# Four-layer gated cross-attention kernel, one core: the last mixture of experts of batches 1 and 2 by sorted pages of tokens instead of densely

## The chip, the cores and the metric

The kernel runs on one core of a Trainium2 chip, as one launch. The time is the device time of that core in microseconds. TensorE is written PE, its weight loads PEld, VectorE DVE, ScalarE ACT, GpSimd POOL and SyncE SP. TensorE is granted one of two clock levels, 1.2 or 2.4 GHz; the profile prints the mean grant as a share of the higher one.

## What is computed

Four batches (B = 4) of S = 512 tokens with D = 128 features pass through four layers; each adds a gated cross-attention and a gated feed-forward part. The change touches the feed-forward part of the last layer, here called moe_3: a mixture of 64 experts of which each token uses six, and a shared expert.

```python
x = x + jnp.tanh(g_ffn[3]) * _L3_ffn_ref(_layernorm(x, axis=-1), ...)

def _moe_forward(...):                       # HIDDEN 128, INTER 64, E 64, K 6, G 8, TG 4
    shared = jax.nn.silu(x @ sg_w.T) * (x @ su_w.T) @ sd_w.T
    scores = jax.nn.sigmoid(x @ gate_w.T) + gate_bias
    group_scores = scores.reshape(T, G, E // G).max(axis=-1)
    ...                                      # keep the 4 best groups of 8 experts
    topk_w, topk_i = lax.top_k(masked_scores, K)
    topk_w = topk_w / (topk_w.sum(axis=-1, keepdims=True) + 1e-08)
    comb = jnp.zeros((T, E), x.dtype).at[jnp.arange(T)[:, None], topk_i].add(topk_w)
    h = jax.nn.silu(jnp.einsum('th,eih->eti', x, eg_w)) * jnp.einsum('th,eih->eti', x, eu_w)
    routed = jnp.einsum('eti,ehi,te->th', h, ed_w, comb)
    return shared + routed
```

## The kernel before

The program is a sequence of blocks; at a block's end all engines meet. In a block each engine has its own instruction stream, written in Python as a generator that yields step numbers. `interleave` (L691) merges the stream of the main work with those of side works: after the main work yields step n, every side whose next step is due at n or earlier goes on. So a side's instructions stand in program order between those of the main work, on every engine, and an engine that waits in a side's instruction also holds up the main work queued behind it.

After the first layers come, for each batch b, the blocks `attention_2` (L1524) and `attention_2f` (L1904). The rest of layer 2 and the attention of layer 3 is `back` (L2173): a chain of 33 steps in which PE, ACT, DVE and POOL take turns on one PSUM bank. For batches 0 to 2 it runs in the block `backs` (L2684), all three side by side, between the two parts of the attention of batches 2 and 3. For batch 3 it is a side of the third moe_3 block, one step per item. Its norms use POOL for the power of -0.5.

`moe_3` (L2454) is dense. It treats the shared expert and 32 pairs of experts as 33 items. For each item PE makes the gate and the up product for all 512 tokens (`up`, L2479, two matmuls with 512 columns), ACT takes the silu (L2528), DVE multiplies by the up product (`used_3`, L2566) and by the token's share for that expert, which is zero where it isn't chosen (`gated_3`, L2574), and PE adds the down product into one bank (`down`, L2498, four matmuls with 128 columns). The shares come from a routing prologue on DVE (L2535 to L2556), are turned by PE (L2495), written to the DRAM tensor `gates3` and read back broadcast over the partitions (`spread_gates_3`, L2431, SP's queue). Expert weights are loaded anew for each batch in eight chunks of gate, up and down (`load_experts_3`, L2421); the first four chunks of the next batch are loaded at the end of a block. The next batch's layernorm is a side at steps 32 to 34 (`norm_ahead`, L642), and PE is kept busy with products that nobody reads (`keep_turning`, L630).

Layer 1's mixture is already done by pages: `route_1` (L1048) sorts two batches' tokens by expert on chip (ranks by matmuls with triangular and all-one matrices), POOL scatters the normed rows to DRAM (L1182, one indirect DMA for 128 rows), `pages_1` (L1196) loads pages of 128 rows, each of one expert, and uses that expert's weights at an address held in a register (L1253, L1270); `combine_1` (L1468) gathers the results back (L1476).

Of the kernel before, what the change touches and what calls it, by code (L numbers as in the profile page):

```python
# [44 lines left out]
FRONT_SMALL = 884  # L45
HID = 4
# [7 lines left out]
ROUND_MAGIC = 1.5 * 2.0 ** 22  # L54
LN2 = float(np.log(2.0))
# [7 lines left out]
def flamingo_kernel(nc, a, at, early_at, out):  # L63
    with ExitStack() as ctx:
# [17 lines left out]
        found_1 = [ctx.enter_context(nc.semaphore(f"rows_found_{b}")) for b in range(B)]  # L82

# [190 lines left out]
        back_2 = dict(**back_wide(region_b), **back_rest(region_a, 0))  # L274
        back_3 = dict(**back_wide(region_c), **back_rest(region_a, 1280))
        back_w2, back_w3 = back_norm(region_a, 2560), back_norm(region_a, 3840)
# [72 lines left out]

        hid = part(turned, 0, [P, HID, F1])  # L350
# [42 lines left out]
        made_1 = [nc.dram_tensor(f"made_1_{g}", (PAGES * P, D), FP32, kind="Internal").ap() for g in range(2)]  # L393

# [1129 lines left out]
        def attention_2(k, b, combined=None, last=None):  # L1524
# [75 lines left out]
            with nc.Block() as block:  # L1600
                @block.sync
                def _(sp):
                    clear_set(sp, 1 - k % 2)
                    if last:
                        last.sync(sp)

# [566 lines left out]
        def back(s, b, bk, bk_sum, w, f):  # L2173
# [217 lines left out]
            def gpsimd(pool):  # L2391
# [16 lines left out]
                 "hu", "hc", "y", "dve", "x", *LOADS, *AHEAD)  # L2408

        def load_gate_3(sp, s, c):  # L2410
            sp.dma_start(eg3[:, c, :], a["eg3"][:, c, :]).then_inc((s.load0, s.load1, s.load2, s.load3)[c % 4], 16)  # L2411

        def load_up_3(sp, s, c):
            sp.dma_start(eu3[:, c, :], a["eu3"][:, c, :]).then_inc((s.load0, s.load1, s.load2, s.load3)[c % 4], 16)

        def load_down_3(sp, s, c):
            lo = ed3_lo + 4 * D * c
            sp.dma_start(ed3[:, 4 * c:4 * (c + 1), :].rearrange("p c d -> p (c d)"),
                         a["weights"][:, lo:lo + 4 * D]).then_inc((s.load0, s.load1, s.load2, s.load3)[c % 4], 16)

        def load_experts_3(sp, s, chunks):  # L2421

            loads = (s.load0, s.load1, s.load2, s.load3)
            for c in chunks:
                if c >= 4:
                    sp.wait_ge(loads[c % 4], 48 * (c // 4))
                load_gate_3(sp, s, c)
                load_up_3(sp, s, c)
                load_down_3(sp, s, c)

        def spread_gates_3(sp, s, s_next=None):  # L2431
# [5 lines left out]
            for n in range(4 * CH3):  # L2437
# [6 lines left out]
                if n % 4 == 1 and n // 4 < 4:  # L2444
                    load_experts_3(sp, s, (4 + n // 4,))
                if s_next and n in (18, 21, 24, 27):
                    sp.wait_ge(s.y, 17)
                    load_experts_3(sp, s_next, ((n - 18) // 3,))
# [5 lines left out]
        def moe_3(s, b):  # L2454
# [18 lines left out]
            def tensor(pe):  # L2473
# [5 lines left out]
                def up(i):  # L2479
# [4 lines left out]
                    else:  # L2484
                        c, at_row = (i - 1) // 4, P * ((i - 1) % 4)
                        if at_row == 0:
                            pe.wait_ge(loads[c % 4], 48 * (c // 4 + 1))
# [18 lines left out]
                for i in range(n_items + 2):  # L2506
# [6 lines left out]
                    if i == n_items + 1:  # L2513
# [76 lines left out]
            return record(tensor=tensor, vector=vector, scalar=scalar, gpsimd=gpsimd)  # L2590

# [79 lines left out]
        def attention_2f_then_moe_3(b, b_next):  # L2671
            k = next_block()
            s_next = sems(1 - k % 2, MOE_3)

            def early_loads(sp, s):
                sp.wait_ge(s.o, 3)
                for c in range(4):
                    load_gate_3(sp, s_next, c)
                sp.wait_ge(s.o, 4)
                for c in range(4):  # L2680
                    load_up_3(sp, s_next, c)
            attention_2f(k, b, xs[b_next], copy_xnt, None, early_loads)

        def backs():  # L2684
# [4 lines left out]
            s_ahead = sems(k % 2, AHEAD, s_of[-1])  # L2689
# [149 lines left out]
```

## Time and profile before

| | us |
| --- | --- |
| median of 3 runs (lowest to highest) | 1861.17 (1857.43 to 1866.37) |
| the profiled execution, its whole time | 1862.18 |
| its span, first to last instruction | 1860.4 |
| mean granted clock of PE in it | 0.948 |
| PE busy, of the span | 1671.0 (90%) |
| DVE busy | 1175.6 (63%) |
| ACT busy | 771.9 (41%) |
| POOL busy | 750.9 (40%) |

In the page of the profile, the second part cuts the span into 40 slices of 46.5 us and prints the busy share of each engine in tenths. The last nine slices are the four moe_3 blocks: PE at 9, POOL at 0, DMA at 3 to 6. The shares of busy time are for the whole span, the blocks are bound in different ways, and what the change is worth has to be read from its blocks.

### The profile page before, as it was taken

To read this page: it belongs to the slowest core of one execution; us is meant where nothing else is said; L and a number is where in the kernel's file an instruction comes from. 1 tells how busy PE (TensorE), PEld (TensorE's weight loads), DVE (VectorE), ACT (ScalarE), POOL (GpSimd) and SP (SyncE) were. 2 spreads that over 40 slices of the span, in tenths; PEclk is the share of its full clock that TensorE was granted. 3 is DMA by queue.
4 is the path that set the end of the run, shared out by engine and by line. 5 is a ranking of instruction groups with operands and counts; after the bars stand their busy time and mean duration, and the time that the engine had idled before them with its cause. 6 is when DMAs were issued, how large, how long until landed. Compare 5 with 4: busy or idle time off the path is not lost. (4 is left out here: it accounts for less than half of the span.)

```text
span 1860.4 us, 30824 instructions
## 1 busy us (share of the span) xinstructions
PE 1671.0 (90%) x10277; PEld 1113.9 (60%) x10277; DVE 1175.6 (63%) x3054; ACT 771.9 (41%) x1957; POOL 750.9 (40%) x976
## 2 busy tenths in 40 slices
PE   5755699899999899999999979699999999999999
PEld 4545377657756477565676654457756565656656
DVE  6857568867666477564775653757656555554655
ACT  2321254346537466273662643146627322232321
POOL 2441744347666287471874750026646100000000
PEclk7866799999999999999999988899999999999999
DMA  9010122100000000000000000000000564634352
GB/s 334 19 29 1 40 88 77 32 10 9 1 1 2 2 11 1 1 2 1 10 4 1 2 1 0 1 1 1 2 1 24 168 192 127 194 105 127 112 173 85
DMA packets 63964, 92.51 MB, mean 50 GB/s; under 512 B 11192, under 2 KB 29240, under 8 KB 63040
## 3 DMA queue, kind: packets, MB, share of 16 engines
q1 hardware_dynamic: 61760, 86.34, 15.1%
q0 software_dynamic: 2048, 4.20, 0.8%
q8 instruction: 85, 1.39, 0.3%
q14 instruction: 71, 0.58, 0.1%
HBM read 80.55 MB, written 9.96 MB: 49 GB/s over the span
## 5 line engine op out<-in xcount | busy, mean ns | idle before, releaser
L1617 POOL TENSOR_TENSOR rows<-rows,rinv 128x512 f32<-128x512 f32 x192 | 198.5, 1061 | 117.4 <-DVE rinv L1857 117.4
L2528 ACT ACTIVATE region_b<-psum 128x512 f32<-128x512 f32 x132 | 78.8, 597 | 259.4 <-PE psum L2490 259.4
L1781 ACT ACTIVATE rows<-psum,nmax 128x512 f32<-128x512 f32 x192 | 129.9, 682 | 123.5 <-DVE nmax L1850 123.4
L2502 PEld LDWEIGHTS psum<-region_c,region_b 128*128 128x128 f32 x1024 | 132.1, 192 | 56.8 <-issue 43.9
L2566 DVE TENSOR_TENSOR region_b<-region_b,psum 128x512 f32<-128x512 f32 x128 | 87.8, 686 | 123.7 <-ACT region_b L2528 121.3
L1849 DVE TENSOR_REDUCE lg<-psum 128x2 f32<-128x1024 f32 x128 | 155.7, 1216 | 3.3
L1966 POOL TENSOR_TENSOR rows<-rows,rinv 128x128 f32<-128x128 f32 (+2 forms) x192 | 127.1, 684 | 75.6 <-DVE rinv L2135 75.6
L2130 DVE TENSOR_REDUCE nmax<-psum 128x1 f32<-128x128 f32 (+3 forms) x256 | 113.7, 486 | 40.8 <-PE psum L2012 39.8
L1861 DVE COPY turned<-psum 128x512 f32<-128x512 f32 x128 | 88.2, 689 | 80.5 <-PE psum L1677 79.5
L1665 PE MATMUL psum<-region_a,region_b 64*128 64x256 f32 x1024 | 130.6, 392 | 5.9 <-ACT rows L1781 2.9
L2502 PE MATMUL psum<-region_c,region_b 128*128 128x128 f32 x1024 | 133.7, 276 | 1.7 <-DVE region_b L2574 1.7
L2489 PE MATMUL psum<-xnt,region_a 128*128 128x512 f32 x256 | 132.0, 597 | 0.0
L2490 PE MATMUL psum<-xnt,region_a 128*128 128x512 f32 x256 | 130.8, 592 | 0.0
L1698 PE MATMUL psum<-turned,region_a 128*64 128x256 f32 x1024 | 124.7, 386 | 0.4
L2009 PE MATMUL psum<-region_a,region_b 64*128 64x128 f32 (+2 forms) x896 | 104.5, 346 | 11.2 <-ACT rows L2082 5.3
L1665 PEld LDWEIGHTS psum<-region_a,region_b 64*128 64x128 f32 x1024 | 93.0, 187 | 28.7 <-ACT rows L1781 7.7
L1677 PEld LDWEIGHTS psum<-weights,rows 128*128 128x128 f32 x768 | 82.0, 140 | 44.8 <-issue 24.9
L1677 PE MATMUL psum<-weights,rows 128*128 128x128 f32 x768 | 103.3, 279 | 3.8 <-ACT turned L1790 2.4
L2082 ACT ACTIVATE rows<-psum,nmax 128x128 f32<-128x128 f32 (+2 forms) x192 | 96.0, 509 | 10.4 <-DVE nmax L2130 10.4
L1698 PEld LDWEIGHTS psum<-turned,region_a 128*64 128x64 f32 x1024 | 68.7, 137 | 47.0 <-issue 19.6
L1790 ACT ACTIVATE turned<-psum 128x512 f32<-128x512 f32 x128 | 76.5, 598 | 46.2 <-PE psum L1677 46.2
L616 POOL TENSOR_SCALAR rtmp<-mv 128x4 f32<-128x4 f32 x3 | 0.7, 227 | 223.7 <-DVE mv L609 223.7
(747 smaller groups left out, 3619.7 us busy)
## 6 DMA issues: line engine op xcount, KB each, us to landing
pt<-gates SPq DMA_DIRECT2D x128, 128.0 KB, 3.2
ysb<-gates SPq DMA_DIRECT2D x128, 128.0 KB, 3.5
region_a<-in_eg SPq DMA_DIRECT2D x32, 256.0 KB, 3.5
region_a<-in_eu SPq DMA_DIRECT2D x32, 256.0 KB, 3.6
region_c<-in_weights SPq DMA_DIRECT2D x32, 256.0 KB, 4.8
sorted<-kctx SPq DMA_DIRECT2D x2, 1536.0 KB, 14.6
region_b<-sorted SPq DMA_DIRECT2D x12, 256.0 KB, 3.5
made<-rows SPq DMA_DIRECT2D x12, 256.0 KB, 2.4
```

The lines of the kernel that those rows point to most:

```text
L1617: nc.gpsimd.tensor_tensor(row(u, j), row(u, j), rinv[:, 2 * u + j:2 * u + j + 1].broadcast_to([P, S]), ALU.mult).then_inc(s.pn, 1)
L1665: mm = nc.tensor.matmul(s_bank(u, j)[:, 256 * half:256 * (half + 1)], qtt[lo:lo + 64, p, P * t:P * (t + 1)], ktt[lo:lo + 64, p, 256 * half ...
L1677: mm = nc.tensor.transpose(turn_bank(place(n, i))[:, P * k:P * (k + 1)], row(u, j)[:, P * k:P * (k + 1)], ident[:, :])
L1698: nc.tensor.matmul(bank(7)[lo:lo + HD2, 256 * half:256 * (half + 1)], vtok[:, k, P * p + lo:P * p + lo + HD2], turned2[:, 2 * half + j, k, :],
L1781: nc.scalar.activation(row(u, j), s_bank(u, j), ACT.Exp, bias=nmax[:, 2 * u + j:2 * u + j + 1], accum_out=sum_column(u // T, u % T, j)).th ...
L1849: link(nc.vector.tensor_reduce(maxima(u // T)[:, both(u), 0], both_scores(u), AX.X, ALU.max, negate=True))
L1966: nc.gpsimd.tensor_tensor(head, head, rinv[:, 2 * u + j:2 * u + j + 1].broadcast_to([P, keys(u)]), ALU.mult).then_inc(s.pn, 1)
L2009: nc.tensor.matmul(s_bank(u, j)[:, cols], qtt[lo:lo + 64, p, P * t:P * (t + 1)], krot[lo:lo + 64, cols], start=(h == 0), stop=True, skip_g ...
L2130: nc.vector.tensor_reduce(nmax[:, 2 * u + j:2 * u + j + 1], s_bank(u, j)[:, 0:keys(u)], AX.X, ALU.max, negate=True).then_inc(s.mx, 1)
L2489: nc.tensor.matmul(bank(i % 2), wg, w.xnt[:, :], start=True, stop=True)
L2490: nc.tensor.matmul(bank(2 + i % 2), wu, w.xnt[:, :], start=True, stop=True).then_inc(s.g, 1)
L2502: mm = nc.tensor.matmul(bank(7)[:, P * t:P * (t + 1)], htb[:, i % 2, P * t:P * (t + 1)], wd, start=(i == 0 and t == 0), stop=(i == n_items ...
```

## The change

Batches 1 and 2 no longer have a dense moe_3 block each. Their 1024 tokens are sorted by expert into pages of 128 rows: `QUADS_3 = (6*8 + 64)//4 = 28` groups of four pages, always all 112 pages, whatever the routing.

- The block `backs` gets on SP the loads of batch 0's eight gate chunks, and at its end (steps 33 and 35) batch 0's layernorm as a side. That layernorm leaves the last `attention_2f`.
- Batch 0's dense moe_3 moves ahead of the last `attention_2`, directly behind `backs`. Its side is `route_3`: layernorm of 8 token tiles, logits, choice of six of 64, ranks and starts of the experts' pages, 48 indirect DMAs that scatter the normed rows to `sorted_3`, the owners of the pages, the shares, and the shared expert for both batches.
- SP copies zero rows into `sorted_3` during batch 1's `attention_2` (`fill_rows_3`, 14464 rows of 512 B, and 128 rows more).
- The last `attention_2f` gets the loads of the first three groups of pages and of all gate and up chunks; the next block begins with the loads of all down chunks.
- The block `pages_3` has batch 3's `back` as a side, slowed by `paced` so that its step n is due at page 2n (one step for every two pages), and batch 3's layernorm at pages 67 to 70.
- The last block is batch 3's dense moe_3, with the expert weights still resident and without loads; its side `combine_3` gathers the made rows by 48 indirect DMAs and adds them by 48 DVE operations at steps 14 to 19 and 27 to 32.
- `back_2` and `back_3` get other places in `region_a`; `keep_turning` leaves the last block.

```diff
+GROUP_3 = (1, 2)
+GT3, K6 = 2 * T, 6
+QUADS_3 = (K6 * GT3 + E3) // 4
+PAGES_3 = 4 * QUADS_3
...
+        def route_3(s, bk, bk2):
...
+            def vector(dve):
+                link = chained(dve, s.chain)
+                yield 0
...
+                for j, rows in enumerate(tiles):
+                    nc.vector.bn_stats(stats_3[:, j, :], rows).then_inc(s.stat, 1)
...
+                yield 1
+                dve.wait_ge(s.rstd, 2)
+                for j, rows in enumerate(tiles):
+                    nc.vector.tensor_scalar(xn_3[:, j, :], rows, mv_3[:, j, 0:1], rstd_3[:, j:j + 1],
+                                            ALU.subtract, ALU.mult).then_inc(s.xn, 1)
...
+                    link(nc.vector.tensor_tensor(share_of, from_3, best_3[:, :, k:k + 1].broadcast_to(wide), ALU.is_equal))
+                    link(nc.vector.tensor_tensor(share_of, share_of, comb_3, ALU.mult))
+                    yield (17, 18, 20, 22, 23, 24)[k]
+                    link(nc.vector.tensor_reduce(shares_3[:, k, :], share_of, AX.X, ALU.add))
...
+                pool.wait_ge(s.slots, 1)
+                for j in range(GT3):
+                    for k in range(K6):
+                        nc.gpsimd.indirect_dma_start(sorted_3[:, :], bass.IndirectOffsetOnAxis(ap=slots_3[:, j, k:k + 1], axis=0),
+                                                     xn_3[:, j, :], None).then_inc(scattered_3, 16)
...
+        def pages_3(s, s_late):
+            gate_up = region_a[:, 0:2 * CH3 * 512].rearrange("p (a n) -> p a n", a=2)
+            TURN_LAG, DOWN_LAG = 2, 3
...
+                def up(q, j):
+                    if j == 0:
+                        owners[q] = nc.tensor.value_load(owner_quad3[0:1, q:q + 1], min_val=0, max_val=E3 ** 4 - 1)
+                        pe.wait_ge(s.xtc, q + 1)
...
+                        if q == 0:
+                            pe.wait_ge(s.up_in, 16 * 2 * CH3)
+                    at_expert = (owners[q] // E3 ** j) % E3 * I3
+                    mm = nc.tensor.matmul(up_bank(q)[:, P * j:P * (j + 1)].rearrange("p (a n) -> p a n", a=2),
+                                          page_t3[:, q % 2, P * j:P * (j + 1)], gate_up[:, :, bass.ds(at_expert, I3)],
+                                          start=True, stop=True)
...
+                def down(q, j):
+                    if j == 0:
+                        pe.wait_ge(s.thc, q + 1)
...
+                    at_pair = (owners[q] // (2 * E3 ** j)) % (E3 // 2) * D
...
+                for k in range(PAGES_3 + 4 * DOWN_LAG):
+                    q, j = k // 4, k % 4
+                    if k == 0:
+                        turn_rows(0)
+                    if q < QUADS_3:
+                        up(q, j)
+                    if 0 <= q - TURN_LAG < QUADS_3:
+                        turn_hidden(q - TURN_LAG, j)
+                    if 0 <= q - DOWN_LAG:
+                        down(q - DOWN_LAG, j)
+                    if j == 2 and q + 1 < QUADS_3:
+                        turn_rows(q + 1)
+                    yield k
...
+            def scalar(act):
...
+                for k in range(PAGES_3 + 4 * DOWN_LAG):
+                    q, j = k // 4, k % 4
+                    if k == 0:
+                        copy_rows(0)
+                    if j == 0 and 0 <= q - 1 < QUADS_3:
+                        silu(q - 1)
+                    if j == 0 and 0 <= q - 1 - TURN_LAG < QUADS_3:
+                        copy_hidden(q - 1 - TURN_LAG)
+                    if j == 2 and q + 1 < QUADS_3:
+                        copy_rows(q + 1)
+                    yield k
...
+        def paced(side, at_step):
...
+            block_of(k, pages_3(s1, s_late).sync, pages_3(s1, s_late),
+                     [paced(back(s2, B - 1, bank(6), bank(7), set_f, back_1), lambda n: 2 * n),
+                      norm_ahead(s1, xs[B - 1], set_m, bank(6), copy_xnt, 2 * 33 + 1, 2 * 35)], first_loads)
...
             elif b == 2:
                 attention_2f(next_block(), b)
                 backs()
+                moe_3_beside_route()
             else:
-                attention_2f_then_moe_3(b, 0)
-        moe_3_block(0, first=True)
-        moe_3_block(1)
-        moe_3_block(2, b_back=3)
-        moe_3_block(3)
+                attention_2f_then_pages_3(b)
+        pages_3_beside_back()
+        moe_3_last()
```

In `pages_3` DVE multiplies the silu of a group by its up product (`used`, 256 columns), writes it into one of two halves by the owner's parity (`to_half`, 512 columns) and copies the sums out (`copy_sum`, 512 columns); SP stores each group of pages (256 KB) and loads the next but two (256 KB).

## Rows read from the trace of the kernel before

**Rows 1.** Windows, the four moe_3 blocks: window, length, busy per engine (count), clock, DMA, GB/s.
```profile
1454.40:1549.50 95.10, 93.14 (x416) 57.81 (x416) 50.80 (x96) 23.83 (x38) 1.25 (x2) 0.98 0.56 173
1549.50:1644.50 95.00, 93.17 (x416) 57.59 (x416) 50.80 (x96) 23.84 (x38) 1.26 (x2) 0.98 0.56 160
1644.50:1765.10 120.60, 112.87 (x524) 70.99 (x524) 68.80 (x155) 34.97 (x53) 5.26 (x10) 1.00 0.41 126
1765.10:1860.40 95.30, 92.05 (x412) 57.38 (x412) 48.62 (x84) 23.24 (x37) 0.00 (x0) 0.98 0.42 126
```

**Rows 2.** Groups by line on PE, third block: busy us, mean ns | idle before, releaser.
```profile
L2489 PE MATMUL psum<-xnt,region_a 128*128 128x512 f32 x64 | 33.3, 602 | 0.0
L2502 PE MATMUL psum<-region_c,region_b 128*128 128x128 f32 x256 | 33.3, 275 | 0.0
L2196 PE MATMUL psum<-turned,weights 128*128 128x512 f32 (+1 forms) x20 | 10.5, 609 | 2.1 <-DVE rows L2326 2.1
```

**Rows 3.** Timeline inside layer 1's pages: start, us, engine, line, operation.
```profile
296.36 0.60 PE L1261 MATMUL psum<-weights,turned 128*128 128x128 f32 x4
296.56 0.60 ACT L1305 ACTIVATE turned<-psum 128x512 f32<-128x512 f32 x1 [1.11 <-PE psum L1253]
296.64 1.14 DVE L1372 SCALAR_TENSOR_TENSOR rows<-rows,rstd,region_c 128x128 f32<-128x128 f32 x4 [0.66 <-POOL rstd L1415]
...
296.80 1.06 PE L1270 MATMUL psum<-region_a,turned 128*128 x8
297.06 0.59 ACT L1298 ACTIVATE turned<-psum 128x512 f32<-128x512 f32 x1
...
297.69 1.02 PE L1253 MATMUL psum<-region_a,region_b 128*128 x2
```

**Rows 4.** Address arithmetic in the instruction queues: ns min/median/max, first and last start.
```profile
L1344 DVEq FUSED_REGOPS  x48: 123/156/177, 250.5 to 360.2; - x48
...
L1270 PEldq FUSED_REGOPS  x192: 46/46/51, 237.3 to 355.3; - x192
```

**Rows 5.** Timeline of POOL, two of layer 1's scatters in a row.
```profile
264.08 0.96 POOL L1182 DMA_INDIRECT sorted<-region_c,slots  x1 [0.30 <-issue]
265.34 0.96 POOL L1182 DMA_INDIRECT sorted<-region_c,slots  x1 [0.30 <-DVE rows L1344]
```

**Rows 6.** Timeline around the end of the first moe_3 block.
```profile
1544.57 0.86 DVE L606 BATCH_NORM_STATS2 stats<-x 128x6 f32<-128x128 f32 x4
...
1546.11 1.03 POOL L617 TENSOR_TENSOR rstd<-rtmp,neg_half 128x4 f32<-128x4 f32 x1
...
1547.17 1.12 DVE L627 TENSOR_SCALAR xn<-x,mv,rstd 128x128 f32<-128x128 f32 x4 [0.52 <-POOL rstd L617]
...
1549.57 1.28 ACT L2519 ACT_TABLE_LOAD   x1 [0.26 <-PEq L707]
...
1550.86 0.38 ACT L2519 ACTIVATE lge<-psum 128x256 f32<-128x256 f32 x1
...
1553.28 0.61 DVE L2548 MAX8 m8b<-lg 128x8 f32<-128x64 f32 x4
```

**Rows 7.** The page's costliest groups, DVE's product of 512 columns.
```profile
L2566 DVE TENSOR_TENSOR region_b<-region_b,psum 128x512 f32<-128x512 f32 x128 | 87.8, 686 | 123.7 <-ACT region_b L2528 121.3
```

**Rows 8.** Timeline of SP's queue around the end of the last attention_2f block.
```profile
1450.80 1.75 SPq L2414 DMA_DIRECT2D region_a<-in_eu  x4
...
1454.39 1.75 SPq L2418 DMA_DIRECT2D region_c<-in_weights  x4
```

**Rows 9.** Windows with a full DMA queue or a half idle PE, columns as in rows 1.
```profile
236.00:244.00 8.00, 8.00 (x57) 6.42 (x57) 5.40 (x17) 5.77 (x11) 2.20 (x3) 1.00 0.89 320
...
276.00:284.00 8.00, 4.20 (x27) 3.02 (x26) 3.46 (x13) 2.66 (x5) 6.60 (x9) 1.00 0.10 33
284.00:292.00 8.00, 8.00 (x42) 5.79 (x41) 7.30 (x30) 2.53 (x5) 2.95 (x5) 0.79 0.46 132
...
1196.00:1204.00 8.00, 2.17 (x8) 1.43 (x8) 7.66 (x14) 2.22 (x4) 0.00 (x0) 0.50 0.00 0
```

More of the change, by code:

```diff
@@ L350, in flamingo_kernel, with found_at_3 @@
+        hid_m, hid_t3 = part(region_b, 1024, [P, 2, 8, I3]), part(region_b, 2048, [P, 2, 4 * P])
+        def found_at_3(i, k, t):
+            n = (i * K6 + k) * T + t
+            return part(wide_2, D * n, [P, D]) if n < 32 else part(rows2, D * (n - 32), [P, D])
         hid = part(turned, 0, [P, HID, F1])
@@ L2592, in flamingo_kernel, with slowed, of_engine @@
+        def paced(side, at_step):
+            def slowed(program):
+                def of_engine(eng):
+                    for n in program(eng):
+                        yield at_step(n)
+                return of_engine
+            return record(tensor=slowed(side.tensor), vector=slowed(side.vector), scalar=slowed(side.scalar),
+                          gpsimd=slowed(side.gpsimd))
         block_at = [0]
@@ L2693, in moe_3_block, with moe_3_beside_route @@
-        def moe_3_block(b, b_back=None, first=False):
+            block_of(k, sync, sides[0], [*sides[1:], norm_ahead(s_ahead, xs[3], set_f, bank(6), keys_of(3), 4, 8, LN_EPS),
+                                         norm_ahead(s_first, xs[0], set_m, bank(7), copy_xnt, 33, 35)])
+        def moe_3_beside_route():
             k = next_block()
             s3 = sems(k % 2, MOE_3)
-            s2 = sems(k % 2, BACK, s3)
-            last = b == B - 1
-            sides = [] if b_back is None else [back(s2, b_back, bank(6), bank(5), set_f, back_1)]
-            if not last:
-                sides.append(norm_ahead(s3, xs[b + 1], set_m, bank(4), copy_xnt, 32, 34))
+            sr = sems(k % 2, ROUTE_3, s3)
@@ L2702, in first_loads @@
             def first_loads(sp):
                 for c in range(4):
-                    load_down_3(sp, s3, c)
+                    load_up_down_3(sp, s3, c)
             def sync(sp):
-                spread_gates_3(sp, s3, None if last else sems(1 - k % 2, MOE_3))
-                store(sp, s3, b)
-                if last:
-                    sp.wait_ge(stored, 16 * B)
-            block_of(k, sync, moe_3(s3, b), sides, first_loads if first else None)
+                spread_gates_3(sp, s3, True)
@@ L2713, in flamingo_kernel, with moe_3_last, sync @@
+        def moe_3_last():
+            k = next_block()
+            s3 = sems(k % 2, MOE_3)
+            combined = combine_3(sems(k % 2, LATE_3, s3))
+            def sync(sp):
+                spread_gates_3(sp, s3, False)
+                combined.sync(sp)
+                store(sp, s3, B - 1)
+                sp.wait_ge(stored, 16 * B)
+            block_of(k, sync, moe_3(s3, B - 1, False), [combined])
         fronts_beside_setup()
```

442 lines of the change are left out of this document (404 added, 38 removed).

## The prediction, made before the changed kernel was run

> **What bounds the kernel now.** I read the page first: the last nine slices have PE at 9 tenths while DVE is at 5 or 6, ACT at 2 and POOL at 0. The windows of the four moe_3 blocks say the same per block [rows 1]: the first, second and last take 95.1, 95.0 and 95.3 us, in which PE is busy for 93, DVE for 51 and ACT for 24 us; the third, beside batch 3's back, takes 120.6. The groups by line [rows 2] say of what PE's time consists: 64 matmul passes each for the gate and up products with 512 columns, and 256 passes with 128 columns. The dense blocks are bound by PE's columns and nothing else, and most of what PE does there is multiplied by a zero share. The change removes PE work from the bound engine, so it acts on the path; what has to be found is what takes PE's place.
>
> **What goes.** The second and third blocks: 95.0 + 120.6 = **215.6 us** [rows 1]. In them batch 3's back is worth 120.6 - 95.0 = 25.6 us, of which 112.87 - 93.17 = 19.7 are PE's work and the rest waits. It comes back below.
>
> **The block of pages.** First PE's work. In layer 1's pages four transposes take from 296.36 to 296.80, 0.11 us each, and eight passes of 128 columns from 296.80 to 297.69, also 0.11 each [rows 3]. A group of four pages has 4 + 4 transposes and 4 up and 4 down products of two passes each: 24 x 0.11 = 2.7 us. 28 groups: 75 us, against 2 x 86 for the items of two dense blocks (33 items in 95 us less some 9 of prologue and end, 2.61 us each).
>
> Each product has an address worked out from a packed number by division and remainder. The nearest row is DVE's, 0.156 us for such a term [rows 4]; PE's own plain addresses take 0.046 [rows 4]. Two per page are 0.31 us at the upper price, and PE works 0.64 us on a page, so in a run of matmuls the arithmetic is hidden; the cover is gone behind a wait. I take 0.15 us once per group, bounds 0 and 0.6.
>
> Then the chain across engines. PE turns group q+1 at the end of page j=2; ACT copies it, takes the silu of group q, then copies the hidden rows of group q-2, in this order, and only then may `down` of that group go on. From rows: the four transposes end 0.60 us after their start, ACT starts 0.04 to 0.1 later, copies of 512 columns follow each other at 0.50 and last 0.60 (ACT at 296.56 and 297.06) [rows 3], one of 256 columns takes 0.38 [rows 6], so 0.38 stands for the silu. So `down` may start at 0.65 + 0.50 + 0.38 + 0.60 + 0.05 = 2.2, with the address 2.3 us after the transposes started. Behind it PE still has a down (0.22) and the pages j=1 and j=2 (0.54 each): 3.6 us until the next group's transposes. PE fills only 2.7 of them, and the loop goes at **3.6 us per group**: 28 x 3.6 = 101. DVE has 0.4 + 0.69 + 0.69 = 1.8 us in a group [rows 7] and stays hidden; 512 KB of loads and stores in 3.6 us are 146 GB/s, where the dense blocks move up to 173 [rows 1]. The last three groups drain without new pages, about 7 us.
>
> At the start the up chunks are late. SP issues four of them in 1.75 us from 1450.80, 3.6 us before the next block begins [rows 8]; now it issues eight there, 2 MB, and eight down chunks behind them. At the 320 GB/s of a full queue [rows 9], 2 MB in 6.6 us with some 2 to land, they are in at about 1459, and PE would want them at 1455.5: +4, with block start and end 6 in all.
>
> Batch 3's back has the same 19.7 us of PE work. Every second step falls into the 0.9 us hole that PE has behind the transposes, so I hide 10; but ACT's 11 us of it (34.97 - 23.84 [rows 1]), with loads of the activation tables at 1.28 [rows 6], lie on the chain that paces the loop, and a step of the back is now two pages, about 2.2 us, in place of 120.6/33 = 3.6 us, with the same round trips in it. I take +24, bounds 12 and 45. The block: 6 + 101 + 7 + 24 = **138 us**. Its own bounds: groups at 2.9 us (PE alone with small waits) and a cheap back 105, groups at 4.3 and a dear one 165.
>
> **The first dense block with the routing beside it.** PE's part: 8 transposes 0.9, 8 logit products 1.8, rank products 2.8, the shared expert for two batches 4 x 0.87 + 8 x 0.22 = 5.2; 10.7 us. DVE's part: about 35 operations on 512 columns at 0.69 [rows 7], 24; statistics and norms of 8 tiles 2 x (0.86 + 0.4 + 1.12) = 4.8; 32 searches at 0.15 = 4.9 [rows 6]; some 20 small ones at 0.2, 4: **38 us**. The block has 95.1 - 50.8 = 44 us of DVE to spare, but in 33 equal portions of 1.3, while the routing comes in lumps: steps 0, 1, 4, 5, 6 and 9 bring 2.2 to 3 us each, step 1 also waits for POOL's power (1.03 us and more for the wider one [rows 6]). The lumps overrun by about 16 us together, of which the lags of two items swallow some: +10. Late chunks at the start (up and down are now both loaded there) +2, and the tail with the next layernorm goes, -2. **+21 us**, bounds +9 and +38; 116 us for the block.
>
> POOL's 48 scatters follow each other at 1.26 us [rows 5]: 60 us, and they can't start before the slots are there, at step 10, some 46 us in. They end at 107, nine before the block: hidden, and the first thing to come up if the routing gets faster. By the Trainium skill (SBUF — State Buffer, Who interferes with whom, and the note on SWDGE above it) DVE copies that hold the shared port keep GpSimd from writing descriptors, with a DMA of 0.62 us taking some 3.1; by that figure 48 scatters would last 149 us. In rows 5 the scatters keep 0.96 us beside a busy DVE, so the rule doesn't show here and gets little weight.
>
> **The rest.** Batch 0's layernorm was hidden behind the end of attention_2f; at the end of backs nothing hides it: statistics 1.3, POOL 1.3, norm 1.12, transposes 0.6, copy 0.6 and the hand-overs [rows 6]: +5. In the last block DVE gets 48 additions at 0.28 us (four in 1.14 [rows 3]), 1.1 us in each of twelve steps that have 1.3 to spare, and 24 gathers take 30 us before step 14, which comes at about 44: +2. The zero rows are written by SP in a block where its queue is empty: 0, at most +3. Loads that leave the dense blocks were hidden, 0.
>
> **Sum.** -215.6 + 138 + 21 + 5 + 2 = -49.6, on the profiled execution 1862.2 - 49.6 = 1812.6; the median is 1.0 lower than that execution: **1811.6 us**, 2.7% faster.
>
> **Rivals.**
> *The ACT chain doesn't pace the pages*, because ACT's copies and PE's waits overlap more than I allow: groups at 2.9 us, 28 x 0.7 = 20 less: 1792. For it: PE's transposes and matmuls in layer 1's pages leave no gap. Against: there a hidden tile has a whole page of 2.2 us for its copy. Chance 0.2.
> *The back at two pages per step is too tight.* PE and ACT stand in its round trips while pages wait behind them; each of 33 steps costs 0.6 us more, +20: 1832. For it: in the dense block PE waited 2.1 us for L2326 [rows 2] though a step was 3.6 us long. Chance 0.13.
> *The routing block.* The lumps aren't swallowed, or the scatters start late and end the block: +15: 1827. Chance 0.12.
> *The clock.* In the loop PE stands 0.9 us of each 3.6 and the granted clock falls to its lower level, 1.2 GHz. Then PE's 2.7 us become 5.3, and with the waits that are left a group takes 6.3: +76 for the pages and 20 for the back: about **1905, slower than before**. It decides from 5.4 us per group on, (3.6 + 49.6/28), where the gain is gone. For it: PE with 2.2 of 8 us of work had 0.50 of the clock, and 0.79 in the 8 us behind a window with 4.2 [rows 9]. Against: in that window itself, half idle, the clock was still 1.00 [rows 9], and the loop works 2.7 of 3.6 us in short pieces. The Trainium skill (TensorE: Matmul & The Clock Gate, HAM oscillation) reports loops that micro-idle in this way and fall to the lower clock; by it the loop would be at 1905. Chance 0.05.
> My forecast has 0.5.
>
> **Range.** The ends of all terms together are -215.6 + 105 + 9 + 3 + 0 and -215.6 + 165 + 38 + 8 + 6, that is 1763 and 1863, and they hardly all come at once. 1778 to 1846 takes in the two near rivals on either side and leaves out the clock and the double misfortunes, together 0.2. About 0.5% is what a measurement of this kernel can tell from no change; faster by more than that 0.92, within 0.03, slower 0.05.
>
> **What would show it.** In the trace after: the block of pages lasts 125 to 150 us with PE at about 75% in its last third, where the back is over, transposes of rows at 3.6 us from each other, and `down` at j=0 waiting for ACT's copy (if it waits for nothing, the first rival). In the routing block PE waits for DVE, 116 us in all, and the last scatter ends before the last item. The clock stays at 1.00 in the pages. If a group takes over 5 us, or the routing block over 135, the prediction fails.

## The result, and the profile after

The changed kernel took 1888.52 us (median of 4 runs, 1887.31 to 1889.38) where the kernel before took 1860.56 (4 runs, 1857.43 to 1866.37): a ratio of 1.0157, 95% interval [1.0139, 1.0174]. It is 28 us slower; I had said 50 us faster, 1811.6 us, with 1846 as the upper end of the range. The profiled execution (1887.31 us, span 1885.5) in windows, columns as in [rows 1]; they are the routing block, the block of pages and the last block:

```profile
1211.90:1328.00 116.10, 107.76 (x474) 67.54 (x474) 83.13 (x210) 28.46 (x44) 51.38 (x55) 0.96 0.43 140
1572.40:1791.70 219.30, 145.47 (x791) 120.97 (x791) 69.81 (x156) 52.79 (x102) 5.11 (x10) 0.81 0.27 80
1791.70:1885.50 93.80, 89.60 (x404) 55.59 (x402) 61.13 (x132) 22.48 (x37) 46.30 (x48) 0.98 0.51 135
```

Against [rows 1] the first block grew from 95.1 to 116.6 us (my sum: 116) and the last one shrank from 95.3 to 93.8. The block of pages is what went wrong: 219.3 us where I had 138, a little more than the 215.6 of the two dense blocks that it replaces. PE is busy for 145 us of it, at a clock of 0.81, and DMA moves 80 GB/s: nothing there is full.

What PE and SP's queue wait for in that block (us in total, times, longest us; SP's line is from the answer on the whole span, where only this block has L2889):

```profile
PE psum L2899 <- DMA weights<-sorted: 50.9, 22, 3.7
PE psum L2935 <- ACT region_b L2970: 11.7, 15, 3.2
PE psum L2911 <- DMA region_a<-in_eu: 4.5, 1, 4.5
...
SPq L2889 <- DVE weights L3002: 184.9, 28, 23.7
```

In 22 of 28 groups PE waits for the rows of its pages (L2899 are the transposes that read them), although there are three buffers. One group behind the end of the back, timeline (start, us, engine, line, operation, idle before and its releaser; rows that the argument doesn't need are left out, here and in the timelines below):

```profile
1734.00 0.83 PE L2899 MATMUL psum<-weights 128*128 128x128 f32 x4 [2.37 <-DMA weights<-sorted]
1734.87 0.60 ACT L2957 ACTIVATE weights<-psum 128x512 f32<-128x512 f32 x1 [5.88 <-PE psum L2899]
1735.36 0.38 ACT L2963 ACTIVATE region_b<-psum 128x256 f32<-128x256 f32 x1
1735.63 0.60 ACT L2970 ACTIVATE region_b<-psum 128x512 f32<-128x512 f32 x1
1735.78 0.42 DVE L2987 TENSOR_TENSOR region_b<-region_b,psum 128x256 f32<-128x256 f32 x1 [5.50 <-ACT region_b L2963]
1736.23 0.69 DVE L2995 TENSOR_TENSOR region_b<-region_b,small_f 128x512 f32<-128x512 f32 x1
1736.84 0.68 DVE L3002 COPY weights<-psum 128x512 f32<-128x512 f32 x1
1737.55 0.36 SPq L2889 DMA_DIRECT2D made<-weights  x1
1737.95 0.51 SPq L2855 DMA_DIRECT2D weights<-sorted  x1
1741.08 0.43 PE L2899 MATMUL psum<-weights 128*128 128x128 f32 x1 [2.40 <-DMA weights<-sorted]
```

This is a closed loop. The transposes at 1734.00 release ACT's copy, silu, DVE's `used` and `to_half`, and behind them, in DVE's order, `copy_sum` at 1736.84: 2.84 us. It ends 0.71 later at SP's store (L2889), the load (L2855) is issued 0.40 behind the store, and 3.13 us later its rows are there and the next transposes go: 2.84 + 0.71 + 0.40 + 3.13 = 7.08 us, which is the period. `pages_3.sync` puts into SP's queue load(q), store(q-4), load(q+1), store(q-3) and so on, and store(n) waits for `copy_sum`(n). So load(q+1) can't be issued before `copy_sum`(q-4), which DVE does at the beginning of group q, while PE wants these rows at the third page of group q. The buffer has been free for long: SP stands 184.9 us before the stores, with the loads behind them.

### The profile page after: what moved, and what is told of

Read it like the earlier page. It is cut to its first block and busy times, and to the rows that moved or that the text cites. A ratio compares the mean times of both kernels' runs of the same rounds, so it can differ in the third digit from the quotient of the medians.

```text
span 1885.5 us, 30971 instructions
## 1 busy us (share of the span) xinstructions
PE 1623.1 (86%) x10175; PEld 1112.9 (59%) x10175; DVE 1170.9 (62%) x3120; ACT 771.5 (41%) x1974; POOL 846.1 (45%) x1075
## 5 line engine op out<-in xcount | busy, mean ns | idle before, releaser
L1720 PEld LDWEIGHTS psum<-region_a,region_b 64*128 64x128 f32 x1024 | 92.8, 186 | 28.9 <-ACT rows L1836 7.7
L1732 PE MATMUL psum<-weights,rows 128*128 128x128 f32 x768 | 103.3, 279 | 3.8 <-ACT turned L1845 2.4
L2579 ACT ACTIVATE region_b<-psum 128x512 f32<-128x512 f32 x66 | 39.4, 597 | 141.2 <-PE psum L2541 141.2
L2064 PEld LDWEIGHTS psum<-region_a,region_b 64*128 64x128 f32 x896 | 70.0, 189 | 33.6 <-issue 11.8
L2987 DVE TENSOR_TENSOR region_b<-region_b,psum 128x256 f32<-128x256 f32 x28 | 11.8, 421 | 119.4 <-ACT region_b L2963 119.4
L2079 PE MATMUL psum<-weights,rows 128*128 128x128 f32 x448 | 76.8, 281 | 6.9 <-DVE region_a L2196 1.6
L2553 PEld LDWEIGHTS psum<-region_c,region_b 128*128 128x128 f32 x512 | 66.0, 192 | 28.2 <-issue 23.0
L2957 ACT ACTIVATE weights<-psum 128x512 f32<-128x512 f32 x28 | 16.7, 597 | 149.5 <-PE psum L2899 149.5
L1698 PE MATMUL psum<-kvt,weights 128*128 128x512 f32 x128 | 65.9, 644 | 11.2 <-PEq L760 7.5
```

The lines of the kernel that those rows point to most:

```text
L1720: mm = nc.tensor.matmul(s_bank(u, j)[:, 256 * half:256 * (half + 1)], qtt[lo:lo + 64, p, P * t:P * (t + 1)], ktt[lo:lo + 64, p, 256 * half ...
L1732: mm = nc.tensor.transpose(turn_bank(place(n, i))[:, P * k:P * (k + 1)], row(u, j)[:, P * k:P * (k + 1)], ident[:, :])
L2064: nc.tensor.matmul(s_bank(u, j)[:, cols], qtt[lo:lo + 64, p, P * t:P * (t + 1)], krot[lo:lo + 64, cols], start=(h == 0), stop=True, skip_g ...
L2553: mm = nc.tensor.matmul(bank(7)[:, P * t:P * (t + 1)], htb[:, i % 2, P * t:P * (t + 1)], wd, start=(i == 0 and t == 0), stop=(i == n_items ...
```

## The experiments

The runs fell on four chips, numbered 0, 1, 5 and 10. The chip of the first measurement is called A; its number isn't recorded, so it may be one of the four. Three lengths are taken from every trace: from the first logits product of the routing block to the first transposes of pages (routing block and last attention, "front"), from there to the last logits product of the last block, about 1 us into it ("pages"), and from there to the end ("last"). The times are medians of four or five executions; those marked with a star are of a single one.

| kernel | chip | us | before there | front | pages | last |
|---|---|---|---|---|---|---|
| changed kernel | A | 1888.5 | 1860.6 | 361.4 | 218.4 | 93.7 |
| store q-7 | 0 | 1918.5 | 1866.0 | 409.8 | 145.5 | 144.3 |
| one step per three pages | 0 | 1988.5 | 1866.0 | 409.4 | 218.9 | 143.7 |
| filler on PE | 0 | 1994.0* | 1866.0 | 409.8 | 223.8 | 144.3 |
| stores from POOL | 0 | 1931.9* | 1866.0 | 410.0 | 156.0 | 143.5 |
| changed kernel again | 1 | 1996.3 | 1868.1 | 408.5 | 221.2 | 140.9 |
| store q-7, ACT's order | 1 | 1913.6 | 1868.1 | 409.3 | 145.8 | 143.0 |
| store q-5 | 1 | 1916.3* | 1868.1 | 409.4 | 147.0 | 143.8 |
| store q-7, POOL held | 1 | 1846.2 | 1868.1 | 374.7 | 148.8 | 102.7 |
| POOL held alone | 5 | 1898.3* | 1862.0 | 369.3 | 218.8 | 93.5 |
| store q-7, held, three pages | 5 | 1820.2 | 1862.0 | 369.3 | 145.9 | 93.5 |
| store q-7, held, no back | 5 | 1798.0* | 1862.0 | 368.1 | 116.0 | 93.5 |
| store q-7, pauses | 5 | 1834.4 | 1862.0 | 378.7 | 146.5 | 96.4 |
| store q-7 | 5 | 1815.0 | 1858.1 | 361.5 | 146.2 | 93.5 |
| store q-7, pauses | 5 | 1831.8 | 1858.1 | 378.0 | 143.9 | 96.3 |
| store q-7 | 10 | 1918.5 | 1864.1 | 409.4 | 146.6 | 144.1 |
| store q-7, held | 10 | 1846.4 | 1864.1 | 373.7 | 144.8 | 104.5 |
| store q-7, held, three pages | 10 | 1844.7 | 1864.1 | 378.9 | 144.2 | 105.6 |
| the same, ACT's order | 10 | 1841.4 | 1864.1 | 370.4 | 137.3 | 106.1 |

**The order in SP's queue.** One number is changed, so that the store that SP puts behind load(q) is one whose `copy_sum` is long over:

```diff
-                    n = q - DOWN_LAG - 1
+                    n = q - 7
                     if n >= 0:
                         store_rows(sp, n)
-                for n in range(QUADS_3 - DOWN_LAG - 1, QUADS_3):
+                for n in range(QUADS_3 - 7, QUADS_3):
                     store_rows(sp, n)
```

> SP stores group q-7 behind the load of group q, in place of group q-4; nothing else changes. Theory A (SP's in-order queue: the load of group q+1 is issued only after the sums of group q-4 have been copied out, so the three page buffers don't help and each group pays the landing of a load): groups fall from 7.0 to 7.6 us to about 3.6 us where the back is over and to some 4.5 beside it, PE's wait for the page loads (50.9 us) goes to near 0, the pages block from 219 to about 135 us, the whole to 1888 - 85 = about 1803 us (1785 to 1825). Theory B (the low granted clock, 0.75 to 0.9 in the block, is the cause and the loads merely land late): less than 20 us gained, groups at 6 us or more.

The time in all was a miss (1918.5 us, 1917.11 to 1926.84, ratio 1.0303 [1.0253, 1.0353]); the front and the last block had become 48 and 51 us longer, of which below. The block of pages is 145.5 us, against 218.9 and 223.8 in the two kernels with the old order on the same chip. On chip 5, where the dense blocks are as in the first trace, the same kernel took 1815.0 us (1813.35 to 1816.01), 0.9768 of before [0.9751, 0.9785]. The block of pages there, and a piece of its timeline:

```profile
1572.00:1718.00 146.00, 117.46 (x791) 97.25 (x790) 69.35 (x155) 52.91 (x102) 4.86 (x10) 0.93 0.39 118
...
1690.15 0.60 PE L2899 MATMUL psum<-weights 128*128 128x128 f32 x4
1690.79 0.60 ACT L2957 ACTIVATE weights<-psum 128x512 f32<-128x512 f32 x1 [2.37 <-PE psum L2899]
1691.29 0.38 ACT L2963 ACTIVATE region_b<-psum 128x256 f32<-128x256 f32 x1
1691.55 0.60 ACT L2970 ACTIVATE region_b<-psum 128x512 f32<-128x512 f32 x1
1692.39 0.48 PE L2935 MATMUL psum<-region_c,region_b 128*128 x2 [0.22 <-ACT region_b L2970]
1693.83 0.60 PE L2899 MATMUL psum<-weights 128*128 128x128 f32 x4
```

This is the loop of my sum: `down` at j=0 starts 2.24 us after the transposes (I had 2.3) and waits for ACT's copy, and the next transposes come after 3.68 us (I had 3.6). SP now waits 77.4 us for stores, and PE never for rows of pages.

> The dose: SP stores group q-5 where the changed kernel stores q-4, behind the load of group q. If the order in SP's queue sets the page period, the load of the next group is issued one group earlier; a load takes some 2.6 us to land after 0.9 us of issue, less than a group, so that this one step is already enough and groups take 3.7 us, as with q-7. If it is the landing time that counts, with several loads in flight, the gain lies halfway: groups at 5 to 6 us. The time in all is that of the first experiment, or 30 us more.

The dose: 147.0 us of pages, against 221.2 in the unedited changed kernel on the same chip; behind the back the groups take 3.7 us, with one of 4.9 and one of 4.6. One group more of distance is enough, as expected.

The other way to the same end takes the stores out of SP's queue and issues them from POOL's, which is empty in this block:

```diff
-                    if n >= 0:
-                        store_rows(sp, n)
+            def gpsimd(pool):
+                for k in range(PAGES_3 + 4 * DOWN_LAG + 1):
+                    if k % 4 == 0 and 0 <= k // 4 - 1 - DOWN_LAG:
+                        store_rows(pool, k // 4 - 1 - DOWN_LAG)
```

> The stores of the made pages are issued by POOL's queue, each when its group is copied out; SP only loads. Theory A: as with the later stores on SP, 1795 to 1825 us, groups at 3.6 us behind the back. If it is not the order in SP's queue but the latency of a load as such, the groups stay over 6 us and the time above 1865 us.

156.0 us of pages, and behind the back the groups take 3.67 to 3.74 us but for one of 7.4: with the same amount stored, the stores' place in SP's queue is what matters. The block is 10 us longer than with late stores from SP; why isn't shown. The time in all missed for the same reason as above.

**The clock as the cause?** PE gets one more product of 512 columns before the transposes from the 19th group on, which fills its wait:

```diff
+                    if j == 2 and 18 <= q < QUADS_3:
+                        nc.tensor.matmul(bank(7), ident[:, :], region_a[:, 0:512], start=True, stop=True)
                     if j == 2 and q + 1 < QUADS_3:
                         turn_rows(q + 1)
```

> The changed kernel with one product of 512 columns that nobody reads put ahead of the transposes of every page group from the 19th on, where PE waits 2.4 us for the load. Theory A: the granted clock rises towards 1.00 there, but the group stays at 6.3 to 7.1 us, since only PE's short part of the cycle gets faster: 0 to 8 us for the ten groups. Theory B (clock as the cause): these groups fall to 5 us or less, 20 us or more.

A window of 20 us behind the back, first with the filler (chip 0), then the changed kernel run again without it (chip 1, columns as in [rows 1]):

```profile
1780.00:1800.00 20.00, 12.82 (x73) 9.87 (x73) 5.08 (x9) 4.09 (x9) 0.00 (x0) 0.91 0.22 63
...
1780.00:1800.00 20.00, 13.94 (x72) 12.24 (x72) 5.14 (x9) 4.08 (x9) 0.00 (x0) 0.74 0.24 67
```

The clock rose from 0.74 to 0.91, and the groups from there on took 6.9 to 8.4 us, against 7.0 to 7.5 without the filler. The low clock is a consequence of the wait, not its cause.

**The pace of the back.** It takes one step for every three pages:

```diff
-                     [paced(back(s2, B - 1, bank(6), bank(7), set_f, back_1), lambda n: 2 * n),
-                      norm_ahead(s1, xs[B - 1], set_m, bank(6), copy_xnt, 2 * 33 + 1, 2 * 35)], first_loads)
+                     [paced(back(s2, B - 1, bank(6), bank(7), set_f, back_1), lambda n: 3 * n),
+                      norm_ahead(s1, xs[B - 1], set_m, bank(6), copy_xnt, 3 * 33 + 1, 3 * 35)], first_loads)
```

> The changed kernel with batch 3's back taking a step for every three pages in place of two. Theory A: the cycle through SP sets the pace with or without the back, so the block changes by less than 8 us, 1880 to 1895 us. Rival C (PE stands in the round trips of the back because a step of two pages is too short for them): 15 us or more are gained, 1873 us or less.

1988.5 us (ratio 1.0663 [1.0616, 1.071]), a miss by the standstills of that chip again; the pages took 218.9 us, against 221.2 with two pages per step on chip 1.

**The standstills.** The changed kernel was run again beside others on chip 1.

> The changed kernel, run again beside the others. In the four runs so far PE, ACT, DVE and SP stood still together for stretches of 15 to 36 us, in the routing block and in the last block, while POOL issued its 48 indirect DMAs one behind the other; the first trace of the changed kernel had none of this (its routing block took 116.6 and its last block 93.8 us). Theory S (the standstill belongs to the place where the runs are made, not to the edits): this run shows it too, about 1975 to 1995 us, as the kernel with one step per three pages did, and the store 7 groups behind is then worth 60 to 75 us. Theory E (an edit brings it): 1885 to 1892 us as before.

1996.3 us (1987.4 to 1998.47), ratio 1.0681 [1.0638, 1.0724], 1 us above the range given for theory S, which holds. The same program takes 108 us more than on chip A; the kernel before takes 7 more. Inside chip 1 the late store (q-5, one execution) is worth 1996.3 - 1916.3 = 80 us, 74 of them in the block of pages. What such a standstill looks like, in the routing block of the late-store kernel on chip 10:

```profile
1281.71 1.02 PE L2541 MATMUL psum<-xnt,region_a 128*128 128x512 f32 x2
...
1284.33 1.16 PE L2553 MATMUL psum<-region_c,region_b 128*128 128x128 f32 x8 [1.59 <-DVE region_b L2625]
...
1301.81 0.96 POOL L2845 DMA_INDIRECT sorted<-turned,small_f  x1 [0.30 <-issue]
1302.03 0.69 DVE L2625 TENSOR_TENSOR region_b<-region_b,ysb 128x512 f32<-128x512 f32 x1 [12.06 <-remote]
1302.75 33.48 SPq L2495 DMA_DIRECT2D ysb<-gates  x4
...
1303.08 0.96 POOL L2845 DMA_INDIRECT sorted<-turned,small_f  x1 [0.30 <-issue]
...
1318.23 0.60 ACT L2579 ACTIVATE region_b<-psum 128x512 f32<-128x512 f32 x1 [28.55 <-remote]
...
1334.43 0.69 DVE L2625 TENSOR_TENSOR region_b<-region_b,ysb 128x512 f32<-128x512 f32 x1 [31.70 <-remote]
...
1335.17 2.08 PE L2553 MATMUL psum<-region_c,region_b 128*128 128x128 f32 x8 [30.32 <-DVE region_b L2625]
```

POOL goes on at 1.26 us per indirect DMA, while ACT stands for 28.55 and DVE for 31.70 us with the releaser "remote". That is printed where the awaited semaphore was raised but no instruction ended just before. Whose semaphore it is can be found from the program and the trace's list of semaphore updates. The silu at 1318.23 is that of item 17 (the block's items are counted from 0). It waits for PE's up product of the item, the L2541 of 1281.71: its record ends at 1282.73, its semaphore is raised at 1318.21, 35.5 us later. DVE's L2625 at 1334.43 is that of item 16 and waits for the `down` of item 14, the L2553 of 1284.33: its record ends at 1285.49, its semaphore is raised at 1334.31, 48.8 us later.

The same program on chip 5 starts every silu of this block within 0.4 us of the end of its product's record. So what comes late is the completion of PE's products as the others see it, and ACT and DVE stand because they wait for PE. Every "remote" wait in the traces of chips 0, 1 and 10 is of this kind: the semaphore is one that a product of PE raises. PE and SP stand as links of the same chain: they go on when DVE's L2625 is done. SP is not slow at issuing: its row merges four DMAs of 0.44 to 0.60 us each, two from 1302.75 and two from 1335.15, with a wait for DVE between them. In the traces of chips A and 5 no wait is "remote".

Then POOL is held: before every second indirect DMA it waits for the next item of the dense block.

```diff
                 for j in range(GT3):
                     for k in range(K6):
+                        if k % 2 == 0:
+                            pool.wait_ge(dense.hu, min(10 + (K6 * j + k) // 2, 32))
                         nc.gpsimd.indirect_dma_start(sorted_3[:, :], bass.IndirectOffsetOnAxis(ap=slots_3[:, j, k:k + 1], axis=0),
...
                         for t in range(T):
+                            if t % 2 == 0 and i + k + t:
+                                pool.wait_ge(dense.hu, (i * K6 + k) * 2 + t // 2)
                             nc.gpsimd.indirect_dma_start(found_at_3(i, k, t), None, made_3[:, :],
```

> Store 7 groups behind, and POOL waits before every second indirect DMA, in the routing block and in the last one, for the next item of the dense block (two per item, items of about 3 us). Theory 1 (the other engines stand still because POOL issues its indirect DMAs without a pause): the standstills of 15 to 36 us go, the two blocks come back to about 120 and 95 us, and the kernel takes 1805 to 1830 us. Theory 2 (they come from DMA packets, rings or instruction loading whatever POOL's rhythm): the waits stay within 20%, 1900 to 1925 us.

> The changed kernel with its store 4 groups behind, and only POOL held to two indirect DMAs per item of the dense block. If the two causes are independent, the block of pages stays at 221 us (7.0 to 7.5 us per group) and the two dense blocks come to 130 and 103 us, as in the run with both edits: 1915 to 1920 us, 78 less than the changed kernel in this place. If the late stores need the pause to pay, or the other way round, the sum does not add up by over 15 us.

On chip 1, with the late stores, 1846.2 us (ratio 0.9903 [0.9866, 0.9939]). Alone, on chip 5, 1898.3 us: the block of pages stayed at 218.8, as expected, but that chip has no standstills to remove, so whether the two edits add up can't be read from it, and the last block stayed at 93.5. These two came from different chips, so control and edit were then run on one, chip 10:

> Late stores alone (the kernel of the first experiment), as the control in this place for the three others. If the place shows the standstills, 1912 to 1930 us with two dense blocks some 47 us longer; if it shows none, 1810 to 1820 us: 1885.5 us of the first trace of the changed kernel less the 73 us by which the block of pages was shorter.

> Late stores, POOL held to two indirect DMAs per item. Theory 1 (the pause removes the standstills): 1815 to 1850 us whatever the control shows; if the control shows them, 70 us below it. Theory 2 (it was the place): within 10 us of the control.

1918.5 us without, 1846.4 with the hold (ratios 1.0279 [1.0253, 1.0305] and 0.9905 [0.9879, 0.9931]): theory 1, and the hold is worth 72 us. The front falls from 409.4 to 373.7 and the last block from 144.1 to 104.5; these are still 12 and 11 us more than chip 5 shows without the hold. Short waits for late completions of PE are left, none over 6.8 us, and the hold itself costs time: on chip 5 the front is 369.3 with it and 361.5 without.

Is it the tie to the dense block, or the mere pause? POOL waits for nobody here, but writes a small tile three times after every second DMA (`rest` is a chain: each waits for the one before):

```diff
+                        if k % 2 == 1:
+                            for _ in range(3):
+                                rest(nc.gpsimd.memset(pause[:, :], 0.0))
```

> Late stores; POOL is tied to nothing, but after every second indirect DMA it writes a small tile three times, each waiting for the one before (an estimate of 0.5 to 1 us of pause per pair). Theory 1 (the rhythm of 1.26 us without a pause starves the others): the standstills go or fall below a third, and the kernel takes 1840 to 1870 us, the routing block longer because the scatters end later. Theory 2 (only a tie to the dense block's progress ends a standstill, because POOL must stop while the others stand): the standstills stay, each now longer by the pauses, 1905 to 1940 us.

> Late stores alone, the control of this place for the run beside it: 1912 to 1930 us if the standstills are here, as in three places so far.

> Late stores, and POOL pauses after every second indirect DMA without waiting for another engine. With a control beside it now. Theory 1 (rhythm): 1830 to 1850 us though the control is at 1912 or more. Theory 2 (POOL must stop while the others stand, which only a wait for them brings): within 15 us of the control, or above it.

1834.4 and 1831.8 us, but both on chip 5, whose control took 1815.0 without any standstill. There the pauses cost 17 us, since the scatters end later; whether pauses alone would remove a standstill stays open, as it was not run on chip 0, 1 or 10.

**The back beside the pages, and its pace.**

> Late stores and paused POOL, and the fourth batch's back is left out (its work is missing from the result): the block of pages alone. My sum had 28 x 3.6 + 6 + 7 = 114 us for it and 24 for the back. The groups go at 3.67 us from the first to the last: 28 x 3.67 + 13 = 116 us, and the back's price is 149 - 116 = 33 us; the kernel takes about 1813 us. If the pages are slower on their own at the start (loads, clock), 125 us and more, and the back is worth what I gave it.

116.0 us, and behind the first three groups all go at 3.67 to 4.18 (late stores, POOL held; batch 3's result lacks this work): the back costs 146.2 - 116.0 = 30 us on chip 5.

> Late stores and paused POOL, and the back takes one step per three pages again: the step that this change is named for, where the page loop is no longer held by SP. If the round trips of the back cost a fixed time per step (33 steps either way), the block of pages stays within 5 us of 149 and the time within 0.5% of 1846. If one step per two pages is too tight (my rival), a group beside the back has more room now and the block is 10 to 20 us shorter: 1826 to 1836. If the back's steps hide less in the groups left over, up to 10 us slower.

> As before it, with the back at one step per three pages. The blocks of pages were 148.8 us (two) and 145.9 us (three) in two places; the 26 us between the two kernels' times came from the dense blocks, where both have the same program. So here, in one place: within 0.5% of the run with one step per two pages. If three pages per step are really better, 10 to 25 us faster.

1820.2 us on chip 5 (ratio 0.9777 [0.9747, 0.9806]) looked like 26 us for the pace, but the blocks of pages were 145.9 and 148.8. Side by side on chip 10 the two take 1844.7 (0.9885 [0.9858, 0.9912]) and 1846.4 us, with 144.2 and 144.8 us of pages. One step per two or per three pages makes no difference that can be measured.

**ACT's order.** ACT copies the hidden rows before it takes silu:

```diff
-                    if j == 0 and 0 <= q - 1 < QUADS_3:
-                        silu(q - 1)
                     if j == 0 and 0 <= q - 1 - TURN_LAG < QUADS_3:
                         copy_hidden(q - 1 - TURN_LAG)
+                    if j == 0 and 0 <= q - 1 < QUADS_3:
+                        silu(q - 1)
```

> Store 7 groups behind (as in the first experiment) and ACT copies the hidden rows of group q-3 before it takes the silu of group q-1. In the trace of the first experiment a group takes 3.67 us, as my sum had it. If ACT's chain of three paces the group, as my sum says: down starts 0.4 us earlier, 3.3 us per group where the back is over, and 5 to 10 us less in all than the first experiment. If something else paces it (the turn of the hidden rows waits for silu, DVE's product and the halving): the hidden rows come 0.6 us later, 3.67 us or more, same or up to 15 us slower.

> As the run with three pages per step, and ACT copies the hidden rows before it takes silu. Groups without the back's steps went at 3.40 us in place of 3.67 with this order; with one step per three pages more groups have no step to wait for: 2 to 5 us faster than the run with three pages. If the copies in the new order wait longer for PE when a step of the back lies between, no difference.

Groups without a step of the back go at 3.40 in place of 3.67 us (the sum had 3.3), so ACT's chain paces them. With two pages per step the block did not get shorter (145.8 against 145.5 us, chips 1 and 0): beside the back the groups gave it back. With three it is 137.3 against 144.2 us in one place, yet the times, 1841.4 (0.9876 [0.9852, 0.9899]) and 1844.7 us, are too near to tell apart.

## Why the prediction was wrong, point by point

*The step that failed* is the cost of the stores and loads in the block of pages. I had checked what they move (512 KB in 3.6 us, 146 GB/s against 173 in the dense blocks) and never the order in which SP issues them. The missing term is a round trip: `copy_sum`, store, load, landing, 7.08 us per group in place of 3.6. It is worth 218.4 - 146.2 = 72 us (chips A and 5; 221.2 - 147.0 = 74 inside chip 1) of the 77 by which I was too low. With it removed by one number, the kernel takes 1815.0 us on chip 5, 0.9768 of before; my 1811.6 was 0.973 of it. That these are so near is in part luck: the block of pages is still 8 us longer than my 138, and the last block gives back 3.5. Among the rivals none was this one: I looked for what might be late on PE, ACT, DVE and the routing, and took three page buffers for a guarantee that loads are early. The upper bound of the block, 165, was also too low by its own terms: groups at 4.3 and a back of 45 give 6 + 120 + 7 + 45 = 178.

*The groups of pages.* 3.6 us per group: 3.67 once SP is out of the way, with `down` waiting for ACT's copy as the sum had it. Start, groups and tail: 114 against 116.0 us without the back.

*The back*: +24 with bounds 12 and 45; measured 30. The hiding of 10 us of PE's work was too generous. The rival that two pages are too tight fell: three pages give the same.

*Gate chunks at the start*: +4; PE waited 4.5 us for them. *Address arithmetic*: a term of it in PE's queue has a median of 0.12 to 0.13 us (I had taken DVE's 0.156 [rows 4]), and PE's waits in the loop have other releasers.

*The routing block*: +21 and 116 us; 116.6. The parts missed in both directions: PE's work grew by 107.8 - 93 = 15 us (I had 10.7), DVE's by 83.1 - 51 = 32 (38), so the agreement of the sum is in part luck. The last scatter started at 1323.3, 111 us into the block and 5 us before its end (I had the end of the scatters at 107). Scatters kept 0.96 and 1.26 us as in [rows 5].

*The end of the backs*: +5. Now the layernorm of batch 0 stands behind the last addition, 1205.98 to 1211.95, 6.0 us where it was 1.3:

```profile
1205.98 0.75 DVE L2443 SCALAR_TENSOR_TENSOR x<-psum,gate,x 128x512 f32<-128x512 f32 x1 [0.53 <-PE psum L2333]
1206.76 0.87 DVE L659 BATCH_NORM_STATS2 stats<-x 128x6 f32<-128x128 f32 x4
...
1211.95 1.30 PE L2525 MATMUL psum<-weights,xnt 128*128 128x64 f32 x5 [0.93 <-PEq L760]
```

*The last block*: +2; it is 1.5 us shorter than before. The additions and gathers are hidden; why it is shorter isn't shown.

*The clock rival* came nearest in its number (1905 us) and was wrong in its mechanism. It said that holes in PE's work bring the clock down and that this makes the group long. The clock did fall, to 0.74 behind the back, and PE's 117 us of work in the block became 145; but PE still waited for rows at the end of each group, and with the clock raised to 0.91 the groups got no shorter. By the Trainium skill (TensorE: Matmul & The Clock Gate, HAM oscillation) a loop in which PE waits for a DMA in every turn falls to the lower clock; the trace agrees (2.4 of 7.1 us of wait, a mean clock of 0.74), and the filler shows that here the lost clock cost nothing, because it ate only into the wait.

A chance of 0.05 for slower was too small also for a reason that no row of before shows: the same program can be 108 us slower on another chip.

## What to carry to other kernels

SP's queue here is a program in order. For each load ask which wait stands in front of it in its queue, what that wait is released by, and whether this is later than the moment at which the load must be issued; by the program, more buffers with the same order would gain nothing (not run). Bandwidth says nothing about this: here DMA ran at 80 GB/s with PE waiting in 22 of 28 groups. And before two variants are compared, run both on one chip, with the lengths of the blocks beside the times: twice here a difference, of 26 and of over 100 us, belonged to blocks that the edit had not touched. And before an engine is said to be slow, take apart a merged row and ask whose semaphore it waits for: the 33.48 us on SP's row were a wait.

## What the runs showed of the hardware

On chips 0, 1 and 10, while POOL issues 48 indirect DMAs at 1.26 us each, the completions of PE's products come late: 35.5 and 48.8 us behind the end of the product's record in the rows above. ACT, DVE and through them SP and PE stand, up to 36.2 us at a time (ACT, the first late-store run), and without the hold the front and the last block take 47 to 51 us more each. On chips A and 5 the same programs show nothing of it. Holding POOL to two per item of the dense block brought 72 us back on chip 10. POOL's own instructions were not slowed (a median of 0.96 us for the scatters, with and without standstills), and the DMA queues were far from full (70 GB/s from 1303 to 1317 us in the trace of the rows above).

The Trainium skill (SBUF — State Buffer, Who interferes with whom) names the port pair of DVE and GpSimd as the only contention between engines over that memory, and gives PE no share in it. So it doesn't explain that PE's completions come late, and no run here shows which resource is shared. The end of a matmul in the profile is modelled, so the traces don't tell either whether the products or only their signals were late. Why only some chips show it stays open too.
